# P times V one unit later, and exponentials in PSUM with one normalising operation

## The reference

```python
x = x + tanh(g_xattn) * xattn(layernorm(x), ctx_4096, mask, position_bias, ln_weight, w_q, w_k, w_v, w_out)
x = x + tanh(g_ffn) * ffn(layernorm(x), base_W, base_b, router_W, router_b, A, B, expert_map)

# xattn: 32 heads of 128
h = rmsnorm(h, ln_weight)
q, k, v = h @ w_q.T, ctx @ w_k.T, ctx @ w_v.T           # per head
score = softmax(where(mask, q @ k.T + position_bias, -inf)); score = where(mask, score, 0)
return h_in + (score @ v) @ w_out.T
# ffn: a base product, a softmax router over 15 outputs with the best 8 kept,
# and low-rank experts (8 of rank 16), weighted by the router
```

## Time and profile before

| what | value |
|---|---|
| runs | 876.75, 880.88, 875.33 us |
| profiled execution | 884.5 us |
| its span, first to last instruction | 882.3 us |
| mean granted clock of TensorE | 0.984 |
| busy: TensorE, VectorE, ScalarE, GpSimd | 847.7, 699.9, 494.7, 496.1 us |
| DMA | 214.72 MB, mean 243 GB/s |

### The profile page before, as it was taken

How to read it: one execution, slowest core, us unless ns; L and a number is a source line. 1 busy time by engine, 2 the same in 40 slices (tenths; PEclk the granted TensorE clock), 3 DMA queues, 4 the chain that set the end, 5 groups by cost and what they waited for, 6 DMA issues and landing times.

```text
span 882.3 us, 13927 instructions
## 1 busy us (share of the span) xinstructions
PE 847.7 (96%) x4212; PEld 712.1 (81%) x4212; DVE 699.9 (79%) x1172; ACT 494.7 (56%) x1185; POOL 496.1 (56%) x352
## 2 busy tenths in 40 slices
PE   7999999999999998889999999999999999987898
PEld 5887888778888887778888888888888888876786
DVE  6888777877766666568888889889988989899664
ACT  6566776666676753456555555555555555546210
POOL 0353534653465532557576776777667666757422
PEclk9999999999999999899999999999999999999799
DMA  8876677579777785987988888898898898884001
GB/s 291 309 280 246 249 276 274 215 294 360 275 299 274 274 309 156 284 270 227 259 230 264 241 249 255 249 259 252 250 257 246 251 260 253 273 262 140 25 25 72
DMA packets 155392, 214.72 MB, mean 243 GB/s; under 512 B 10960, under 2 KB 109392, under 8 KB 154960
## 3 DMA queue, kind: packets, MB, share of 16 engines
q1 hardware_dynamic: 155344, 214.13, 75.6%
HBM read 128.11 MB, written 85.98 MB: 243 GB/s over the span
## 4 chain that ended last, share of the span: by engine, by line
PE 32%; DMA 24%; DVE 24%; ACT 7%; issue 5%; SPq 4%; POOL 1%; DVEq 0%; ACTq 0%; POOLq 0%
DMA pT<-p_rows 11%; DMA p_rows<-p_blocks 10%; DVE p_norm L1128 6%; PE Sb L1417 4%; PE Sb L1418 4%; PE Sb L1419 4%; ACT p_exp L773 4%; SPq L346 4%; DVE unit_out L950 2%; PE Ab L1417 2%; PE Ab L1418 2%; PE Ab L1419 2%; DVE p_blocks L1134 2%; DVE rscale L1123 2%; DMA v_raw<-wv 2%
## 5 line engine op out<-in xcount | busy, mean ns | idle before, releaser
L495 POOL TENSOR_TENSOR w_lo<-w_raw,w_hi 128x1280 fp32r<-128x1280 f32 (+1 forms) x29 | 84.8, 2924 | 122.7 <-ACT w_hi L639 122.7
L544 POOL TENSOR_TENSOR P_hl<-pT,P_hl 128x512 fp32r<-128x512 f32 x64 | 82.8, 1294 | 103.1 <-ACT P_hl L639 103.1
L539 POOL TENSOR_TENSOR a_rest<-small_a,A_hi 128x512 f32<-128x512 f32 x64 | 89.9, 1404 | 47.3 <-ACT small_a L767 47.1
L639 ACT ACTIVATE P_hl<-pT 128x512 fp32r<-128x512 f32 x64 | 40.5, 633 | 124.7 <-DMA pT<-p_rows 124.7
L773 ACT ACTIVATE p_exp<-s_sb,negmax 128x128 f32<-128x128 f32 x256 | 99.0, 389 | 10.2 <-DVE negmax L1105 9.7
L532 POOL TENSOR_TENSOR bm<-bias,maskneg 128x512 f32<-128x512 f32 x64 | 84.1, 1313 | 17.7 <-DVE s_sb L1111 11.9
L1128 DVE TENSOR_TENSOR p_norm<-p_exp,rscale 128x512 f32<-128x512 f32 x64 | 90.2, 1410 | 2.3
L1588 PE MATMUL Ab<-P_hl,V_hi 128*128 128x256 f32 x256 | 65.8, 335 | 17.6 <-POOL P_hl L544 14.4
L639 ACT ACTIVATE A_hi<-Ab 128x512 fp32r<-128x512 f32 x64 | 38.3, 598 | 67.9 <-PE Ab L1589 67.9
L639 ACT ACTIVATE U<-Sb 128x512 f32<-128x512 f32 x90 | 53.6, 600 | 40.5 <-PE Sb L1419 39.9
L639 ACT ACTIVATE w_hi<-w_raw 128x512 fp32r<-128x512 f32 (+2 forms) x67 | 60.2, 903 | 22.5 <-PE Kb L1419 6.7
(11 more groups left out here) (300 smaller groups left out, 2703.2 us busy)
## 6 DMA issues: line engine op xcount, KB each, us to landing
qk_units<-unit_out SPq DMA_DIRECT2D x128, 512.0 KB, 3.3
qk<-qk_units SPq DMA_DIRECT2D x64, 1024.0 KB, 7.3
p_rows<-p_blocks SPq DMA_DIRECT2D x64, 256.0 KB, 2.7
pT<-p_rows SPq DMA_DIRECT2D x256, 64.0 KB, 4.2
w_raw<-wqk SPq DMA_DIRECT2D x31, 512.0 KB, 4.3
v_raw<-wv SPq DMA_DIRECT2D x32, 256.0 KB, 4.8
o_raw<-wo SPq DMA_DIRECT2D x32, 256.0 KB, 4.7
stage<-ctxT SPq DMA_DIRECT2D x8, 256.0 KB, 5.7
```

The source lines that it names most:

```text
L495: pool.tensor_tensor(w_lo[:, n % 2, first:5, :], w_raw[:, n % 2, first:5, :], f32(w_hi[:, n % 2, first:5, :]), ALU.subtract).then_inc(w1_l ...
L539: pool.tensor_tensor(a_rest[:, :, :], small_a[:, :, :], f32(A_hi[:, r, :, :]), ALU.subtract).then_inc(a_rest_done, 1)
L544: pool.tensor_tensor(blocked(P_hl[:, :, 1, :]), queries(pT[:, r, :, :, :]), f32(blocked(P_hl[:, :, 0, :])), ALU.subtract).then_inc(p_lo_do ...
L639: act.activation(dst, src, ACT.Copy).then_inc(done, 1)
```

## The change

**P times V one unit later.** TensorE's step t applies P of unit t - 3 instead of t - 2, and makes the output product of t - 5 instead of t - 4. What follows from it moves too: `probs_hi` and `probs_lo` to t - 3, `attention_hi`, `small_attention`, `a_remainder` and `attention_lo` to t - 4. `pT` has four places instead of two. A store of blocks now waits until the load of two units before has landed.

**Exponentials in PSUM.** From unit 2 on ScalarE writes the exponentials to the bank QP instead of `p_exp` in SBUF, and one scalar_tensor_tensor on VectorE makes `p_norm` from them, with `valid` as the scalar operand and `rinv` as the second tensor. `rscale` is gone. Since QP is taken, all output products of units up to 58 go to Ob, and TensorE waits for `add_out` of the unit just before instead of the one before that. `add_out` moves to the end of VectorE's step.

**The last group.** `x_plus_gated` moves by one place, `x1`, `x1_stats` and `y` move behind the transposition, the loads of x again and of the base weights move, and the orders behind the last step are written for one more output product and one more P times V.

```diff
@@ -135,7 +135,7 @@
-        p_blocks, pT = sb("p_blocks", [P, Q32, HU, 32]), sb("pT", [P, 2, Q32, HU, 32])
+        p_blocks, pT = sb("p_blocks", [P, Q32, HU, 32]), sb("pT", [P, 4, Q32, HU, 32])
@@ -286,8 +286,9 @@
         def v_bank(t, b):
...
-        def o_bank(b):
-            return (Ob[:, :], QP[:, :])[b % 2]
+        def exp_at(u):
+            return p_exp if isinstance(u, int) and u < EARLY else heads(QP[:, :])
...
         def queries(t):
@@ -297,8 +298,8 @@
-        out_bank = [Ob[:, :], QP[:, :], Ob[:, :], Vb[:, :], Ob[:, :], Vb[:, :], Ob[:, :], Vb[:, :]]
-        yT_bank = [QP[:, :], Kb[:, :]] * 3 + [QP[:, :], QP[:, :]]
+        out_bank = [Ob[:, :], Ob[:, :], Ob[:, :], Vb[:, :], Ob[:, :], Vb[:, :], Ob[:, :], Vb[:, :]]
+        yT_bank = [Kb[:, :], QP[:, :]] * 3 + [QP[:, :], QP[:, :]]
@@ -336,6 +337,9 @@
+                if not (isinstance(g, int) and g == 0 and b < 2):
+                    sp.wait_ge(pt_done[b % 2], 16 * Q32 * (B // 2) * g + 16 * Q32 * (b // 2))
@@ -343,7 +347,7 @@
             def load_blocks(g, b):
...
-                    sp.dma_start(pT[32 * j:32 * j + 32, b % 2, :, :, :].rearrange("c i h r -> c i (h r)"),
+                    sp.dma_start(pT[32 * j:32 * j + 32, b % 4, :, :, :].rearrange("c i h r -> c i (h r)"),
...
             def load_bias(g, q):
@@ -446,16 +450,17 @@
-                    if last and b == 0:
+                    if first and b == 7:
...
+                    if last and b == 0:
...
-                    if last and b >= 2:
-                        sp.wait_ge(f_u, b - 1)
-                        sp.dma_start(x_again[:, b % 2, :], x[:, b, :]).then_inc(ld_x2[b % 2], 16)
-                    if last and b == 3:
+                    if last and 0 < b < 7:
+                        sp.wait_ge(f_u, b)
+                        sp.dma_start(x_again[:, (b + 1) % 2, :], x[:, b + 1, :]).then_inc(ld_x2[(b + 1) % 2], 16)
+                    if last and b == 5:
@@ -557,10 +562,12 @@
             def step(g, b, q):
...
-                a_remainder(t - 3, (b - 3) % 2)
-                probs_lo(t - 2, b % 2)
-                if last and b >= 5:
-                    late_root(b - 5)
+                if not (first and b < 4):
+                    a_remainder(t - 4, b % 2)
+                if not (first and b < 3):
+                    probs_lo(t - 3, (b - 3) % 4)
+                if last and b >= 7:
+                    late_root(b - 7)
@@ -613,14 +618,19 @@
+            a_remainder(UNITS - 4, 0)
+            late_root(1)
+            late_root(2)
+            probs_lo(UNITS - 3, 1)
+            for k in (1, 2, 3):
+                late_low(2 + k, w_base_lo[:, k, :], base_raw[:, k, :], w_base_hi[:, k, :])
+            late_root(3)
...
-            probs_lo(UNITS - 2, 0)
-            late_root(3)
-            late_low(5, w_base_lo[:, 3, :], base_raw[:, 3, :], w_base_hi[:, 3, :])
+            probs_lo(UNITS - 2, 2)
+            late_root(4)
...
-            late_root(4)
...
-            probs_lo(UNITS - 1, 1)
+            probs_lo(UNITS - 1, 3)
@@ -770,13 +780,13 @@
-                    last = act.activation(p_exp[:, i, :], s_sb[:, i, :], ACT.Exp, bias=negmax[:, i:i + 1],
+                    last = act.activation(exp_at(u)[:, i, :], s_sb[:, i, :], ACT.Exp, bias=negmax[:, i:i + 1],
...
             def probs_hi(u, r, pairs):
...
-                act.wait_ge(pt_done[r], 16 * Q32 * pairs)
+                act.wait_ge(pt_done[r % 2], 16 * Q32 * pairs)
@@ -795,10 +805,11 @@
             def step(g, b, q):
...
-                attention_hi(t - 3, (b - 3) % 2)
-                small_attention(t - 3)
+                if not (first and b < 4):
+                    attention_hi(t - 4, b % 2)
+                    small_attention(t - 4)
...
-                probs_hi(t - 2, b % 2, B // 2 * g + b // 2)
+                probs_hi(t - 3, (b - 3) % 4, B // 2 * g + (b - 1) // 2)
@@ -894,14 +905,11 @@
+            v_evict_hi(1, 1)
+            exponentials(2)
+            v_evict_hi(2, 2)
...
-            exponentials(2)
-            v_evict_hi(1, 1)
-            v_evict_hi(2, 2)
-            attention_hi(0, 0)
-            small_attention(0)
...
-            probs_hi(1, 1, 1)
@@ -922,17 +930,21 @@
+            attention_hi(UNITS - 4, 0)
+            small_attention(UNITS - 4)
+            probs_hi(UNITS - 3, 1, UNITS // 2 - 1)
+            for k in (1, 2, 3):
+                late_high(w_base_hi[:, k, :], base_raw[:, k, :])
+            y_hi(0)
...
-            y_hi(0)
-            late_high(w_base_hi[:, 3, :], base_raw[:, 3, :])
-            probs_hi(UNITS - 2, 0, UNITS // 2)
...
+            probs_hi(UNITS - 2, 2, UNITS // 2)
...
-            probs_hi(UNITS - 1, 1, UNITS // 2)
+            probs_hi(UNITS - 1, 3, UNITS // 2)
@@ -1120,17 +1132,15 @@
-                dve.tensor_tensor(rscale[:, :], rinv[:, :], valid[:, b:b + 1].broadcast_to([P, HU]),
-                                  ALU.mult).then_inc(rscale_done, 1)
-                dve.wait_ge(rscale_done, u + 1)
...
-                scale = rscale[:, :].rearrange("p (b o) -> p b o", o=1).broadcast_to([P, HU, S])
-                dve.tensor_tensor(p_norm[:, :, :], p_exp[:, :, :], scale, ALU.mult).then_inc(norm_done, 1)
+                scale = rinv[:, :].rearrange("p (b o) -> p b o", o=1).broadcast_to([P, HU, S])
+                dve.scalar_tensor_tensor(out=p_norm[:, :, :], in0=exp_at(u)[:, :, :], scalar=valid[:, b:b + 1],
+                                         in1=scale, op0=ALU.mult, op1=ALU.mult).then_inc(norm_done, 1)
...
             def transpose_blocks(u):
...
-                reached(dve, p_lo_done, u - 1)
+                reached(dve, p_lo_done, u - 3)
@@ -1140,7 +1150,7 @@
             def add_out(u, b):
...
-                dve.tensor_tensor(acc[:, b, :], o_bank(b), acc[:, b, :], ALU.add).then_inc(acc_done, 1)
+                dve.tensor_tensor(acc[:, b, :], Ob[:, :], acc[:, b, :], ALU.add).then_inc(acc_done, 1)
...
             def x_plus_gated(j):
@@ -1182,19 +1192,20 @@
-                attention_lo(t - 3, (b - 3) % 2)
+                attention_lo(t - 4, b % 2)
...
-                if last and b >= 5:
-                    x1(b - 5)
-                    x1_stats(b - 5)
-                elif not (first and b < 5):
-                    add_out(t - 5, (b - 5) % B)
-                if last and b >= 1:
-                    x_plus_gated(b - 1)
+                if last:
+                    x_plus_gated(b)
...
-                    y(b - 5)
+                    x1(b - 5)
+                    if b == 7:
+                        y(0)
+                    if b > 5:
+                        x1_stats(b - 6)
+                elif not (first and b < 5):
+                    add_out(t - 5, (b - 5) % B)
@@ -1362,14 +1372,17 @@
+            x1_stats(2)
+            y(1)
+            attention_lo(UNITS - 4, 0)
+            y_lo(0)
...
-            y_lo(0)
+            y(2)
...
-            x_plus_gated(7)
+            y_lo(1)
...
-            y_lo(1)
@@ -1536,16 +1549,14 @@
-                    if isinstance(u, int) and u == 1:
-                        pe.wait_ge(first_sum_done, EARLY)
...
-                    elif late and b > 1:
-                        pe.wait_ge(f_x1, b - 1)
+                    elif late and b > 0:
+                        pe.wait_ge(f_x1, b if b < 3 else b - 1)
...
-                        reached(pe, acc_done, u - 1)
+                        reached(pe, acc_done, u)
...
-                    made = product(out_bank[b] if late else o_bank(b), A_hi[:, b % 2, h, :], A_lo[:, b % 2, h, :],
+                    made = product(out_bank[b] if late else Ob[:, :], A_hi[:, b % 2, h, :], A_lo[:, b % 2, h, :],
@@ -1618,22 +1629,19 @@
             def step(g, b, q):
...
-                before = (t - 4, g, b - 4, q) if b >= 4 else (t - 4, g - 1, b + 4, 1 - q)
+                before = (t - 5, g, b - 5, q) if b >= 5 else (t - 5, g - 1, b + 3, 1 - q)
...
-                if not (first and b < 4):
+                if not (first and b < 5):
...
-                if not (first and b < 4):
+                if not (first and b < 5):
...
-                if ends:
-                    y_transpose(0)
-                if not (first and b < 2):
-                    apply_probs(t - 2, (b - 2) % 4)
+                apply_probs(t - 3, (b - 3) % 4)
@@ -1658,12 +1666,9 @@
-            for b in (1, 2):
+            for b in (1, 2, 3):
...
-            apply_probs(0, 0)
-            v_half(3, 0, 3, 0, 0)
-            v_half(3, 0, 3, 0, 1)
@@ -1701,10 +1706,13 @@
+            late_out(3)
+            y_transpose(0)
+            apply_probs(UNITS - 3, 1)
+            y_transpose(1)
...
-            y_transpose(1)
+            lora_and_router(0)
...
-            lora_and_router(0)
...```

How this moves the instructions is seen from each engine's order. VectorE, one step inside the loop over groups, before (`acc<-Ob` is `add_out`, REGISTER_ALU rows only compute counts to wait for):

```order
L1101 TENSOR_TENSOR s_sb<-Sb,bm 128x512
L1103 TENSOR_TENSOR s_sb<-Sb,s_sb 128x512
```

23 lines of the change are left out of this document (10 added, 13 removed).

## The result

| kernel | median us | lowest to highest | runs |
|---|---|---|---|
| before | 880.01 | 872.98 to 883.39 | 16 |
| changed | 875.06 | 872.61 to 877.72 | 16 |

The ratio is 0.9937, with a 95% interval of 0.9917 to 0.9956: 5 us faster, 0.6%. The gain is smaller than forecast (867 us), and the time is inside the range of 858 to 877. The profiled execution of the changed kernel took 874.47 us, near its median. The profiled one of the kernel before took 884.5 us, 4.5 above its median, so a second one was taken later (880.39 us). I compare with both.

A forecast was written before the change was run, and what follows sets the result against it. TensorE, busy 96% of the span, was taken as the bound, losing time to late P and half clocks. Gains of 14.7 less 3.5 at the end gave 11.2 us (884.5 to 873.3 profiled); 10 off 876.75 gave 867, range 858 to 877.

The forecast's parts named there:

- The floor and the two long stretches: Units 11 to 57 and 58 to 62: floor 7.32 us a unit; gains of 5.0 of 5.4 and 5.0 of 5.5 us.
- I take 4.7 whole: Units 8 to 10: the whole 4.7 us lost against the floor goes when P times V comes later.
- I cost it at nothing: Output products in Ob alone: VectorE's addition done at 7.2 to 7.4 of its step, margin 2.2 us, no cost.
- None of this lies on TensorE's path in a steady unit: it is room: PSUM exponentials and one normalising operation: 1.2 us less VectorE work per unit, no gain on TensorE's path.
- p_norm at 0.74: VectorE's normalising operation with one PSUM input takes 0.74 us beside POOL, instead of 1.56 in the mean.
- The end, 3.5 us: Behind the last scores, one more P times V and output product cost 3.5 us, range -1 to 9.
- R + 32.5: P times V of unit 63, counted from the start R of the last scores; R + 29.0 before, what follows unchanged.
- So I take 10 off them: Base of the time: three runs' median 876.75 us holds fewer pauses than the profiled execution; minus 10 gives 867.
- The end at 8 to 13 us: Rival: POOL's queue and the clock make the end cost 8 to 13 us, time 872 to 876; chance 0.23.
- All pauses gone, the start's too: Rival: the end costs nothing and the start gives 3 us more, time 857 to 861; chance 0.10.
- Transfers as the limit: Rival: transfers limit the kernel, the wait moves from P's to qk's loads, time 872 to 875; chance 0.06.
- The slower case, by long exponentials: Rival: doubled exponentials and p_norm at 1.56 push the addition past the 2.2 us margin, 885 up to 890; chance 0.09.

The follow-up runs named there:

- the repeat: The changed kernel timed again with no edit, against the kernel before: 875.21 us, ratio 0.9941.
- Experiment 5: Changed kernel with SyncE's one-off wait for the last q and k stores moved behind the loads of step 7, first group: 872.44 us, ratio 0.9912.
- 9: The kernel of experiment 4 with only SyncE's wait for the last stores moved behind the loads of step 7: 867.05 us, ratio 0.9835.
- experiment 4: Also called P early: kernel before with exponentials in PSUM, one normalising operation, output products in Ob, addition at step's end; P times V undelayed: 870.6 us, 0.9894.
- experiment 3: Changed kernel with exponentials back in SBUF and two normalising operations; delay kept, all output products in Ob: 875.73 us, ratio 0.9934.
- 10: The kernel of experiment 4 with two normalising operations again, exponentials still in PSUM: 874.56 us, ratio 0.9950.
- 11: The kernel of experiment 4 with exponentials in SBUF, read there by one normalising operation: 872.30 us, ratio 0.9914.
- 2: Changed kernel with exponentials in SBUF, two normalising operations, output products in Ob and QP by turns in all groups but the last: 874.54 us, 0.9933.
- 6: Changed kernel with the split of two wv blocks moved behind the exponentials of unit 4: 874.11 us, ratio 0.9926.
- 7: Changed kernel with GpSimd's three low halves of base weights moved behind P's low half of unit 62: 874.92 us, ratio 0.9945.
- 8: The kernel of experiment 4 with SyncE's wait moved and the wv split behind unit 4's exponentials: 866.79 us, ratio 0.9841.
- experiment 12: A second profile of the kernel before, no edit, one execution: 880.39 us.

## Why the prediction was wrong, step by step

**The floor and the two long stretches: right.** 10.0 us were taken, 10.8 and 11.4 came; pitch 7.32 throughout, no wait for P.

**Units 8 to 10, "I take 4.7 whole": failed.** Taken 4.7, given -0.9 and -0.7 (1.0 to 1.2 in the repeat, with 25.64 us). With it failed "I cost it at nothing" for the single bank: the sum of VectorE's step (done at 7.2 to 7.4) let the exponentials begin behind the scores, and left out what stands ahead of them in ScalarE's queue, a split that waits for o_raw. I had seen pT late at 393.97 and did not ask why it was: SyncE's wait. P had more time, but VectorE's results, from the same hole, had none. Experiment 5 shows it (27.49 to 23.95 us), and 9 in the other order (27.21 to 23.08); in the kernel before itself the wait was not moved. In the steady units the bank does cost nothing.

**"None of this lies on TensorE's path in a steady unit: it is room": failed, and is the step that hides most.** It cost the forecast of this change nothing, since the delay already takes the pauses away, but it hid the better change. I read the path of P from the transposed blocks on and took VectorE's time ahead of them as given. But VectorE ran without a pause for scores (its waits for them in the long stretch of before: 0.3 us in all) and 1.1 us behind them. Shortened, it has the blocks 2.9 us earlier, which is enough without the delay (experiment 4). So the two parts of the change are substitutes: each removes the same pauses, and only the delay pays with work behind the last scores.

One rival stands untested. The addition, 0.65 us, moved behind the transposition in every version but the kernel before, and so left the way of P's blocks. They are ready at + 9.8 in the kernel before, at + 8.2 in experiment 3, + 7.7 in 10, + 7.4 in 11 and + 6.9 in 4 (means). No run moved the addition alone or left it in its place, so it is not shown that the PSUM part would be enough without this move, nor excluded that the move would be. For the delay the sum speaks: the latest low half of P came at + 22.4, and with the delay TensorE asks at + 21.4 + 7.32 = + 28.7.

Why VectorE had room under the delay alone too is in this pair of rows of experiment 3, and the pair of the kernel before:

```profile
558.00 1.29 POOL L523 TENSOR_TENSOR v_lo<-v_raw,v_hi 128x512 fp32r<-128x512 f32 x1
...
559.34 0.69 DVE L1140 TENSOR_TENSOR p_norm<-p_exp,rscale 128x512 f32<-128x512 f32 x1
```

```profile
562.52 1.30 POOL L518 TENSOR_TENSOR v_lo<-v_raw,v_hi 128x512 fp32r<-128x512 f32 x1
...
562.63 1.73 DVE L1128 TENSOR_TENSOR p_norm<-p_exp,rscale 128x512 f32<-128x512 f32 x1
```

Before, GpSimd waits for P's high half, its operations come late, and v_lo lies beside p_norm, which takes 1.73 us; so P is late again. By the timeline 38 of 46 p_norm there lie beside a GpSimd operation (1.74 us in the mean) and eight do not (0.69 each). With the delay P is there in time, GpSimd is done before p_norm begins, and all 47 take 0.69, with the exponentials in SBUF. That the late P keeps itself late in this way is my reading of the two traces; no run changed GpSimd's order alone, and the moved addition shifts VectorE against GpSimd too.

**p_norm at 0.74: right** (0.751, each beside GpSimd). The Trainium skill, "SBUF — State Buffer", Who interferes with whom, has a VectorE instruction with one SBUF input, outside the 2-port modes, free of contention with GpSimd, and one with two SBUF inputs in contention with a GpSimd instruction that reads SBUF. The rows agree, 0.75 against up to 1.82 us.

**The end, 3.5 us: the size came near, its working did not.** It cost 1.7 against the first profile and 4.8 against the second, inside -1 to 9. Against the second, TensorE's busy time is 68.20 - 64.31 = 3.9 of it; against the first, which ran at a clock of 0.91, only 68.20 - 67.42 = 0.8. The forecast put all of it ahead of unit 63's P times V, at R + 32.5, and "what follows is unchanged". It came at R + 29.4, 0.5 and 2.0 later than in the two profiles of before, and what follows took 1.3 and 2.8 us more. In experiments 2, 5, 6 and 7, which have the same order there, it took 48.6 to 48.7 us at a full granted clock, and in the changed kernel, its repeat and experiment 3 49.9 with a half clock in it. Why the kernel before had 48.6 with a half clock too is open. So the near hit of the 3.5 is partly luck. And it was a price that need not be paid: P early ends in 71.1 us, and in 71.1 and 73.5 in experiments 8 and 9.

**"So I take 10 off them": failed.** The sum gave 873.3 for the profiled execution, and 874.47 was measured. That this came so near is luck: of the 11.2 us, 5.6 were missing in units 8 to 10, and 4.0 came back from places that the sum had otherwise (1.4 ahead of unit 8, 0.8 from unit 11 to 62, 1.8 of the end). I then took the gain off the median of three runs, 876.75, on the ground that these held fewer of the pauses. Sixteen runs have 880.01, and experiment 12, at 880.39, has the same pauses; no execution near 876 was profiled.

In one line, against the second profile of before: up to unit 8 -0.5, units 8 to 10 -0.7, units 11 to 62 +11.4, the end -4.8, together 5.4 to 5.5 us where 11.2 were forecast. Of the 8.1 us between 867 and 875.06, 3.3 are the base (880.01 - 876.75) and 4.8 the gain (9.75 forecast, 4.95 measured).

**The rivals.** The end at 8 to 13 us: no, 1.7 or 4.8. All pauses gone, the start's too: no, 3.3 us of waiting are left in units 8 to 10 and 5.5 for P in the last part. Transfers as the limit: no, TensorE asks for 257 GB/s and gets it. The slower case, by long exponentials: no, 355 ns. The wait for the addition did come, but in two units only, from the side of a late load.

## What to carry to other kernels

Before you price two remedies for the same wait as a sum, ask whether either one alone ends it: follow the late thing's path back to the engine's first operation on it, not to the place where the trace first names a wait. Where an engine's step is given less slack, list what stands ahead of it in every queue that feeds it, one-off waits of the first steps above all. A median of three runs is no base for a difference of 1% when one profile lies 1% above it.

## What was not expected of the hardware

- Four activations of 128 x 128 with their row sums take 355 ns each into PSUM, and 388 into SBUF. The Trainium skill, "ScalarE: Activation LUTs", Step-by-step: what each stage is for, says that the write to PSUM is the faster one. These rows agree, with 33 ns.
- A VectorE operation of 128 x 512 with two SBUF inputs took 0.69 us alone and 1.74 in the mean beside GpSimd, and in the delayed order, with the addition moved, the contention was gone.
- The scale of 128 x 4, which does almost no work, took 0.16 us alone and up to 1.3 beside GpSimd (mean 0.40, 0.63, 0.78 in before, experiments 10 and 3).
